# Window-attention maxima on one Trainium2 core: local and global scores in separate PSUM banks, the mask written by ScalarE

## The reference

```python
h = layernorm(x);  q, k, v = split(h @ w_qkv)
# local: a query in block n (64 tokens) sees the keys from 32 before it to 31 after it
logits = where(win & valid, q . k_neighbours * scale, -1e9)
out_local  = softmax(logits) @ v_neighbours
# global: every 64th token is a key for all queries of its sequence
out_global = softmax(q . k[::64] * scale) @ v[::64]
x = x + layernorm((out_local + out_global) @ w_out + b_out)
x = x + layernorm(real(ifft(fft(layernorm(x)) @ w)) + bias)
```

## Time and profile before

| | |
|---|---|
| median of 3 runs | 3774.73 us |
| the profiled execution, its own time | 3778.02 us |
| its span, first to last instruction | 3775.7 us |
| mean granted TensorE clock | 0.99 |
| busy: PE, PEld | 3697.7, 2682.5 us |
| busy: DVE, ACT, POOL | 2319.9, 1587.6, 1928.3 us |

### The profile page before, as it was taken

One profiled execution on the slowest core, in us unless ns is written; L12 is line 12 of the kernel. 1 busy time (PEld: TensorE's weight loads), 2 busy tenths in 40 slices (PEclk: granted clock), 3 DMA queues, 4 the chain that ended last, 5 costly groups with the idle time before them and its releaser, 6 DMA issues.

```text
span 3775.7 us, 77146 instructions
## 1 busy us (share of the span) xinstructions
PE 3697.7 (98%) x28480; PEld 2682.5 (71%) x28480; DVE 2319.9 (61%) x5331; ACT 1587.6 (42%) x3094; POOL 1928.3 (51%) x3087
## 2 busy tenths in 40 slices
PE   8999999999999899999999999999999999999997
PEld 6888888888874566666666666666666666666675
DVE  4333333333323567777777777777777777777774
ACT  3222222222220344555555555555555555555554
POOL 0000000000000367777777777777777777777777
PEclk9999999999999899999999999999999999999999
DMA  4554455445556456666666666666666666666651
GB/s 154 191 200 169 165 200 191 166 176 200 184 204 155 96 129 152 151 140 142 144 148 145 139 148 153 151 140 141 144 149 145 139 149 149 152 140 140 144 119 40
DMA packets 421938, 574.34 MB, mean 152 GB/s; under 512 B 41688, under 2 KB 186216, under 8 KB 421624
## 3 DMA queue, kind: packets, MB, share of 16 engines
q1 hardware_dynamic: 413080, 567.94, 57.1%
q10 hardware_dynamic: 8256, 2.16, 0.2%
q0 software_dynamic: 288, 0.08, 0.0%
HBM read 364.74 MB, written 203.23 MB: 150 GB/s over the span
## 4 chain that ended last, share of the span: by engine, by line
PE 62%; POOL 1%; ACTq 1%; ACT 0%; DVE 0%; issue 0%; POOLq 0%
PE ps_misc L995 19%; PE ps_max L915 10%; PE ps_sc L935 6%; PE ps_o L967 6%; PE ps_max L918 5%; PE ps_s L967 4%; PE ps_sc L949 4%; PE ps_o L979 3%; PE ps_s L973 3%; PE ps_sc L1004 1%; ACTq L782 1%; PE ps_sc L924 1%; PE ps_sc L943 1%; ACT qk L759 0%; POOL rsb L696 0%
## 5 line engine op out<-in xcount | busy, mean ns | idle before, releaser
L827 DVE TENSOR_REDUCE mx<-ps_max 128x2 f32<-128x256 f32 (+1 forms) x1365 | 485.0, 355 | 489.8 <-PE ps_max L918 466.7
L759 ACT ACTIVATE qk<-ps_sc 128x384 f32<-128x384 f32 (+1 forms) x1024 | 418.9, 461 | 666.0 <-PE ps_sc L935 663.3
L828 DVE TENSOR_REDUCE mx<-ps_max 128x2 f32<-128x384 f32 (+1 forms) x1365 | 612.6, 449 | 0.0
L915 PE MATMUL ps_max<-ks,qs 97*128 97x384 f32 x2048 | 569.1, 357 | 15.1 <-DVE mx L828 13.1
L915 PEld LDWEIGHTS ps_max<-ks,qs 97*128 97x128 f32 x2048 | 368.6, 192 | 180.9 <-DVE mx L828 127.1
L705 POOL TENSOR_SCALAR_AFFINE_SELECT qk<-qk 128x512 f32<-128x512 f32 (+1 forms) x512 | 298.5, 583 | 282.6 <-ACT qk L759 282.5
L371 PE MATMUL po<-ht_hi,w_hi 128*128 128x512 f32 x1024 | 405.6, 396 | 1.5 <-ACT ht_hi L248 1.5
L371 PE MATMUL po<-ht_hi,w_lo 128*128 128x512 f32 x1024 | 400.3, 391 | 0.0
L371 PE MATMUL po<-ht_lo,w_hi 128*128 128x512 f32 x1024 | 399.8, 390 | 0.0
L772 ACT ACTIVATE v<-ps_sc 128x512 f32<-128x512 f32 x512 | 298.2, 596 | 152.4 <-PE ps_sc L949 150.2
L918 PE MATMUL ps_max<-mask,ident_b 128*128 128x192 bf16 x2048 | 352.9, 254 | 0.0
(11 more groups left out here) (114 smaller groups left out, 7507.5 us busy)
## 6 DMA issues: line engine op xcount, KB each, us to landing
ks<-k_hi_d SPq DMA_DIRECT2D x256, 288.0 KB
qs<-q_hi_d SPq DMA_DIRECT2D x256, 256.0 KB
ks<-k_lo_d SPq DMA_DIRECT2D x128, 288.0 KB
xb<-in_L_attn_x SPq DMA_DIRECT2D x132, 256.0 KB, 3.5
q_lo_d<-o_lo SPq DMA_DIRECT2D x32, 1024.0 KB, 8.7
k_lo_d<-o_lo SPq DMA_DIRECT2D x32, 1024.0 KB, 10.1
qs<-q_lo_d SPq DMA_DIRECT2D x128, 256.0 KB
vw<-v_d SPq DMA_DIRECT2D x128, 256.0 KB, 2.9
```

The lines of the kernel that those rows point to most:

```text
L759: nc.scalar.activation(p_loc[:, i, 2 * hp:2 * hp + 2, lo:MW], ps_sc[n % 2][:, 0:2 * MW].rearrange("p (h n) -> p h n", h=2)[:, :, lo:MW], A ...
L827: nc.vector.tensor_reduce(mx[s % 2][:, 1, h:h + n, tile], ps_max[:, b:b + n, MW:MW + NGLOB], axis=AX.X, op=ALU.max)
L828: last = nc.vector.tensor_reduce(mx[s % 2][:, 0, h:h + n, tile], ps_max[:, b:b + n, 0:MW], axis=AX.X, op=ALU.max)
L915: nc.tensor.matmul(ps_max[:, b, 0:2 * MW], qs[g][0:ROWS_MAX, h, tile * P:(tile + 1) * P], both_keys(g, h, tile), start=True, stop=True)
```

## The change

The three-bank tile `ps_max` is replaced by two banks `ps_ml` for local scores (two heads of 192 columns in each, used in turn by even and odd units) and one bank `ps_mg` for global scores (two heads of 128 columns). A unit on PE becomes two local matmuls of 192 columns, which do not clear the bank but add to what is in it, and then two global matmuls of 128 columns; both pairs load the same two query tiles, so there are again four weight loads. The mask matmuls L918 are gone. In their place a new item `seed` on ACT copies the mask, for two heads at once (128 x 384 values), into the local bank as soon as DVE has reduced it; unit u+2 then adds its scores there. Two matmuls ahead of all units write the mask into the banks for units 0 and 1. DVE always takes both heads at once, first the local half, then the global half, and signals each by itself (`ml_taken`, `mg_taken`): PE's local matmuls of unit u wait for the seed that follows the local reduction of unit u-2, the global ones for the global reduction of unit u-1.

```diff
-        ps_max = pb("ps_max", [P, 3, 512])
+        ps_ml = [pb(f"ps_ml{b}", [P, 2, 256]) for b in range(2)]
+        ps_mg = pb("ps_mg", [P, 4, P])
...
-        MAXIMA = (-12.81, -11.26, -10.56, -9.74, -8.61, -7.49, -6.9, -6.1)
-        TAKEN = 0.12
-        SCORES = (("mt", 0, -4.23), ("loc", 0, -0.65), ("loc", 1, 0.87), ("loc", 2, 1.16), ("loc", 3, 5.18),
-                  ("last", 0, 5.77), ("glob", 0, 1.84), ("glob", 1, 2.44), ("glob", 2, 2.81), ("glob", 3, 5.4))
+        MAXIMA = (-12.98, -11.14, -10.52, -9.53, -8.35, -7.35, -7.13, -6.1)
+        TAKEN = 0.05
+        SEED = 0.55
+        SCORES = (("mt", 0, -3.77), ("loc", 0, -1.32), ("loc", 1, 0.5), ("loc", 2, 0.87), ("loc", 3, 5.22),
+                  ("last", 0, 5.74), ("glob", 0, 1.64), ("glob", 1, 2.01), ("glob", 2, 2.3), ("glob", 3, 5.48))
...
+                items += [(t + at + SEED, "seed", s, n) for n, at in enumerate(MAXIMA)]
...
@@ scalar
+                    u = 8 * s + i
+                    if name == "seed" and u + 2 < 8 * STEPS:
+                        act.wait_ge(ml_taken, u + 1)
+                        nc.scalar.activation(ps_ml[u % 2][:, :, 0:MW], mask[:].rearrange("p (o n) -> p o n", o=1).to_broadcast([P, 2, MW]),
+                                             ACT.Copy).then_inc(seeded, 1)
@@ vector
-                        dve.wait_ge(max_scored, u + 1)
-                        near = high - low == 1
-                        for b, h, n in ((low, 2 * pair, 2),) if near else ((low, 2 * pair, 1), (high, 2 * pair + 1, 1)):
-                            nc.vector.tensor_reduce(mx[s % 2][:, 1, h:h + n, tile], ps_max[:, b:b + n, MW:MW + NGLOB], axis=AX.X, op=ALU.max)
-                            last = nc.vector.tensor_reduce(mx[s % 2][:, 0, h:h + n, tile], ps_max[:, b:b + n, 0:MW], axis=AX.X, op=ALU.max)
-                        last.then_inc(max_taken, 1)
+                        dve.wait_ge(ml_scored, u + 1)
+                        nc.vector.tensor_reduce(mx[s % 2][:, 0, heads, tile], ps_ml[u % 2][:, :, 0:MW], axis=AX.X,
+                                                op=ALU.max).then_inc(ml_taken, 1)
+                        dve.wait_ge(mg_scored, u + 1)
+                        nc.vector.tensor_reduce(mx[s % 2][:, 1, heads, tile], ps_mg[:, 0:2, :], axis=AX.X,
+                                                op=ALU.max).then_inc(mg_taken, 1)
@@ tensor
+                for b in range(2):
+                    nc.tensor.matmul(ps_ml[b][:, :, 0:MW], ident_b[:],
+                                     mask[:].rearrange("p (o n) -> p o n", o=1).to_broadcast([P, 2, MW]), start=True, stop=True)
...
-                        for n, b in enumerate((first, second)):
-                            h = 2 * pair + (b == high)
-                            at_least(pe, max_taken, u - 1 + n)
-                            nc.tensor.matmul(ps_max[:, b, 0:2 * MW], qs[g][0:ROWS_MAX, h, tile * P:(tile + 1) * P],
-                                             both_keys(g, h, tile), start=True, stop=True)
-                        for b in (first, second):
-                            last = nc.tensor.matmul(ps_max[:, b, 0:MW], ident_b[:], mask[:], start=False, stop=True, skip_group_check=True)
-                        last.then_inc(max_scored, 1)
+                        queries = [qs[g][0:ROWS_MAX, 2 * pair + n, tile * P:(tile + 1) * P] for n in range(2)]
+                        keys = [ks[g][0:ROWS_MAX, 2 * pair + n, :] for n in range(2)]
+                        at_least(pe, seeded, u - 1)
+                        for n in range(2):
+                            last = nc.tensor.matmul(ps_ml[u % 2][:, n, 0:MW], queries[n], keys[n][:, tile * P:tile * P + MW],
+                                                    start=False, stop=True, skip_group_check=True)
+                        last.then_inc(ml_scored, 1)
+                        at_least(pe, mg_taken, u)
+                        for n in range(2):
+                            last = nc.tensor.matmul(ps_mg[:, n, :], queries[n], keys[n][:, SPAN:KROW], start=True, stop=True)
+                        last.then_inc(mg_scored, 1)
```

More of the change, by code:

```diff
@@ L580, in attention_phase @@
         y_stored = [sem(f"y_stored{i}") for i in range(TILES)]
-        max_scored, max_taken = sem("max_scored"), sem("max_taken")
+        seeded, ml_scored, ml_taken = sem("seeded"), sem("ml_scored"), sem("ml_taken")
+        mg_scored, mg_taken = sem("mg_scored"), sem("mg_taken")
         sc_scored, sc_exped = sem("sc_scored"), sem("sc_exped")
@@ new lines, in attention_phase @@
+        TAKEN = 0.05
+        SEED = 0.55
+        SCORES = (("mt", 0, -3.77), ("loc", 0, -1.32), ("loc", 1, 0.5), ("loc", 2, 0.87), ("loc", 3, 5.22),
+                  ("last", 0, 5.74), ("glob", 0, 1.64), ("glob", 1, 2.01), ("glob", 2, 2.3), ("glob", 3, 5.48))
+        VALUES = (("pvl", 0, 3.43), ("pvl", 1, 4.14), ("pvl", 2, 7.23), ("pvl", 3, 7.49), ("pvl", 4, 7.98),
+                  ("pvgs", 0, 8.07), ("oc", 0, 8.66), ("sums", 0, 8.91), ("pvgo", 0, 9.2), ("rglob", 0, 9.06),
+                  ("og", 0, 9.62), ("rloc", 0, 13.95), ("ol", 0, 14.07), ("osum", 0, 14.1))
@@ new lines, in attention_phase @@
+        LATE = (("ot", (24.09, 20.31, 19.06, 15.22)), ("otl", (22.15, 22.4, 20.11, 15.25)))
+        OUT_AT = ((8.8, 9.72, 10.39, 10.6), (8.36, 8.94, 9.48, 10.1))
+        FFN_AT = ((24.77, 25.8, 25.91, 26.74), (25.01, 25.41, 25.93, 26.12))
+        TAIL = (("outa", (10.14, 10.48)), ("outs", (10.97, 10.7)), ("rs0", (12.14, 12.25)), ("y", (12.45, 14.89)),
+                ("ya", (13.22, 16.29)), ("x1", (16.27, 17.22)), ("rs1", (16.46, 17.65)), ("x1n", (17.85, 18.74)),
+                ("tr", (19.38, 19.68)), ("trl", (20.87, 20.26)), ("ffna", (26.47, 26.35)), ("ffns", (27.13, 28.5)),
+                ("rs2", (29.09, 29.52)), ("z", (33.77, 35.43)), ("za", (34.1, 35.47)))
@@ L644, in attention_phase @@
         MISC_BEFORE = dict(zip(MISC[1:], MISC[:-1]))
-        def max_banks(u):
-            first, second = 2 * u % 3, (2 * u + 1) % 3
-            return first, second, min(first, second), max(first, second)
         with nc.Block() as block:
@@ L819, in item @@
                         u = 8 * s + i
-                        tile, pair = i // 2, i % 2
-                        low, high = max_banks(u)[2:]
+                        tile, heads = i // 2, slice(2 * (i % 2), 2 * (i % 2) + 2)
                         if i == 0 and s > 1:
                             dve.wait_ge(sc_scored, unit(s - 2, "mt", 0) + 1)
-                        dve.wait_ge(max_scored, u + 1)
-                        near = high - low == 1
-                        for b, h, n in ((low, 2 * pair, 2),) if near else ((low, 2 * pair, 1), (high, 2 * pair + 1, 1)):
-                            nc.vector.tensor_reduce(mx[s % 2][:, 1, h:h + n, tile], ps_max[:, b:b + n, MW:MW + NGLOB], axis=AX.X, op=ALU.max)
-                            last = nc.vector.tensor_reduce(mx[s % 2][:, 0, h:h + n, tile], ps_max[:, b:b + n, 0:MW], axis=AX.X, op=ALU.max)
-                        last.then_inc(max_taken, 1)
+                        dve.wait_ge(ml_scored, u + 1)
[4 more added lines that the diff above has]
+                                                op=ALU.max).then_inc(mg_taken, 1)
                     if name == "sums":
@@ L908, in item @@
                         tile, pair = i // 2, i % 2
-                        first, second, low, high = max_banks(u)
                         if i == 0:
                             pe.wait_ge(st_loaded[g], 160 * (s // GROUPS + 1))
-                        for n, b in enumerate((first, second)):
-                            h = 2 * pair + (b == high)
-                            at_least(pe, max_taken, u - 1 + n)
-                            nc.tensor.matmul(ps_max[:, b, 0:2 * MW], qs[g][0:ROWS_MAX, h, tile * P:(tile + 1) * P],
-                                             both_keys(g, h, tile), start=True, stop=True)
-                        for b in (first, second):
-                            last = nc.tensor.matmul(ps_max[:, b, 0:MW], ident_b[:], mask[:], start=False, stop=True, skip_group_check=True)
-                        last.then_inc(max_scored, 1)
+                        queries = [qs[g][0:ROWS_MAX, 2 * pair + n, tile * P:(tile + 1) * P] for n in range(2)]
[9 more added lines that the diff above has]
+                        last.then_inc(mg_scored, 1)
                     if name == "mt":
@@ L922, in item @@
                         bank_free(n)
-                        pe.wait_ge(max_taken, 8 * s + 8)
+                        pe.wait_ge(mg_taken, 8 * s + 8)
                         nc.tensor.transpose(ps_sc[n % 2][0:8 * TILES, 0:P], mx[s % 2][:].rearrange("p a h t -> p (a h t)"),
```

3 lines of the change are left out of this document (removed).

## The result

The changed kernel takes 3760.34 us, median of 6 runs (3749.61 to 3763.78), beside 3777.36 us for the kernel before (3774.47 to 3780.58, 6 runs). The ratio is 0.9949, 95% interval 0.9933 to 0.9964. It is faster by 17 us where 102 were forecast, and lies outside the range. The profiled execution took 3760.2 us, its span is 3758.4 us.

A forecast was written before the change was run, and what follows sets the result against it. PE's own instructions were taken to bound the steady step. Units -102 us, first units -10 and late moments +10 sum to -102 us, from a profiled span of 3775.7 to 3674; median forecast 3673 us, range 3640 to 3730.

The forecast's parts named there:

- PE's unit: On PE: four matmuls at 0.109, 0.436 us a unit instead of 0.54, over 1024 units -102 us.
- The rival in which the stream sets the turn: On PE: weight loads hidden, 640 columns take 0.30 us a unit; 246 us less, 3529 us, chance 0.04.
- exposed loads: On PE: each pair of matmuls exposes its first load, 0.59 us a unit; 3826 us, chance 0.02.
- What bounds the kernel: Steady step: nothing but PE's own instructions sets the pace; PE busy 998 of 1000 us.
- The start of the phase: First 12 units, PE and DVE taking turns: 1.1 us apart instead of 1.9, -10 us.
- DVE and the price of a seed: DVE: 100 us less busy time from two-head instructions, no gain by itself; ACT: 0.49 us a seed.
- ACT is hidden: ACT: seeds add 3.9 us a step, 15.0 of 18.4 us with DMA issues (82%), hidden on its own.
- the whole sum: Whole kernel: -102 - 10 + 10 = -102 us, median 3673 us, chance 0.71.
- the other moves in the table cost nothing: Due times, with the two mask matmuls at the start: same instructions, same tile-width switches, so no cost.
- 10 us for rare late moments: ACT late or a DMA issue of up to 1.92 us not hidden: +10 us, bounds 0 and +63.
- The walk: One step followed through ACT, DVE and PE: seeds ready 1 us or more ahead, tightest spare 0.3 us.
- half given back: One 0.49 us seed a step delays an exponential PE needs: +63 instead of +10, 3726 us, chance 0.14.

The follow-up runs named there:

- the old table: Changed kernel with all due times of the kernel before, plus seeds 0.55 after their maxima: 3662.55 us (0.9696).

## Why the prediction was wrong

**PE's unit: right in kind, too dear.** Local (192 columns) and global (128) take the same 0.20 us a pair, so the columns do not set the turn of these small float32 matmuls. That the weight load sets it fits, but no run changes the load alone. I took 0.109 from the score pass; it is 0.10. By the shares of the chain with the old table, (10.1% + 8.3%) of 500 us for 500 / 18.43 x 8 = 217 units, a unit with its switches costs 0.424 us, 0.560 before. That is 0.136 less a unit, 1.1 us a step, where the step itself fell by 0.86: the rest went to other blocks. The rival in which the stream sets the turn (0.30) fell, and so did exposed loads (0.59). The Trainium skill's 81 ns for a load and matmul at 128 columns (TensorE: Matmul & The Clock Gate, section Back-to-back issue gap) is below the 100 ns seen here.

**What bounds the kernel: nearly right.** I read that nothing but PE sets the pace of a steady step. Without the DMA issues on ACT's queue the kernel before was 21 us faster, so PE had small waits already.

**The start of the phase: right for the first units.** 1.21 us a unit for 1.1. What follows them had no term: from 1230 to 1300 us the granted clock is 0.60 in the changed kernel, 0.75 before, some 10 us at full clock.

**DVE and the price of a seed: right.** 494 ns for 490, and 111 us less in DVE's reductions (1098 to 986) for 100.

**ACT is hidden: right for the seeds, in the old order.** With that the whole sum can be tested: it gives 3673 us for the change without its new due times, and the run of that kernel took 3663. The sum holds to 10 us because two errors met: the units brought more than their term, and other blocks took some of it (L951, by its share, 1.27 us a step for 1.17).

**The failed step is the table.** The prediction put it as "the other moves in the table cost nothing: same instructions, same switches between tile widths", and gave back 10 us for rare late moments. The new due times cost 98 us in this kernel and 53 in the kernel before, the larger part of it as PE's wait for the exponentials of `loc3` before `glob3`. The walk that should have found it went through one step, the one with `ffn`; the loss lies in the others, where `y`, `outs`, `ot` and one `out` had changed sides with `loc3` or `maxr0`. I had written that ACT is fuller in steps with `tr`, `y` and `x1n`, and did not walk through them.

**The rival that came true in part** is half given back: 3726 us from one late exponential a step, chance 0.14. Its place was right (a `ps_sc` bank that waits for ACT) and its cause was not: I priced one seed of 0.49 us; it was a chain of a reduction, a seed, a copy, two issues and a norm. The condition was there to be read: 1.1 us of DMA issues between `mt` and `loc3` is in the earlier trace rows, and I used it for the landing of the data and for ACT's load, never for what stands behind it.

## What to carry to other kernels

Where each engine follows a written order, the order is part of the change: sort the old and the new table for every kind of step, and list which items have changed sides with one that PE waits for, before pricing anything. Total load does not show it: ACT had 500 us more to do and hid them all in one order, and lost 43 us by them in the other. And count a DMA issue as an instruction on the engine that issues it: here each of the two took some 0.55 us of ACT's queue, and what stood behind them waited. Put it on a queue on which nothing urgent stands behind.

## What the runs showed of the hardware

**A short wait and the clock.** In the changed kernel PE's clock fell at times in the steady part, which it did not do in the kernel before: mean 0.981 against 0.990. One place (columns as in the earlier trace rows, granted clock third from the end):

```profile
2720.00:2730.00 10.00, 10.00 (x92) 7.82 (x88) 7.48 (x18) 6.62 (x15) 7.61 (x13) 1.00 0.93 227
2730.00:2740.00 10.00, 8.63 (x65) 6.41 (x63) 4.61 (x10) 5.11 (x12) 6.84 (x10) 0.73 0.48 104
2740.00:2750.00 10.00, 10.00 (x57) 6.16 (x55) 5.05 (x11) 3.61 (x8) 5.63 (x11) 0.50 0.64 142
2750.00:2760.00 10.00, 9.24 (x76) 7.39 (x73) 6.30 (x13) 6.28 (x13) 2.30 (x4) 0.91 0.13 39
```

```profile
2732.66 0.50 PE L951 MATMUL ps_sc<-qs,ks 99*128 99x512 f32 x1 [1.37 <-ACT qk L758]
```

PE stood still for 1.37 us before `glob3`, after 30 us without a gap; then the clock goes to the lower of its two levels (0.50, 1.2 GHz) for some 17 us, in which each turn nearly doubles. The fall begins at about 2734.6 and the three windows hold 5.4 + 10 + 1.8 us of it. The length of the wait does not decide it. From 1450 to 3660 us PE waits 29 times for 1.18 us or more before `glob3`, and three of these waits were followed by a fall: the longest (1.66 us, at 1965.60), this one, and one of 1.19 us, after which the clock was low for some 7 us. A longer one, 1.31 us, was not followed by any; the clock there stays at 1.00:

```profile
2043.32 0.50 PE L951 MATMUL ps_sc<-qs,ks 99*128 99x512 f32 x1 [1.19 <-ACT qk L758]
...
2351.22 0.50 PE L951 MATMUL ps_sc<-qs,ks 99*128 99x512 f32 x1 [1.31 <-ACT qk L758]
```

```profile
2045.00:2050.00 5.00, 5.00 (x42) 3.85 (x44) 2.84 (x6) 2.62 (x6) 4.79 (x7) 0.52 0.79 177
...
2350.00:2500.00 150.00, 145.39 (x1435) 109.66 (x1436) 111.08 (x237) 103.77 (x222) 115.73 (x182) 1.00 0.65 148
```

What these runs don't show is what decides. But a stall can cost more than its length. The means differ by 0.009 of 3758 us, 34 us of full clock; some 18 of them lie between 1230 and 1450 us, at the start of the phase (0.60 for 0.75 over 70 us, 0.92 for 0.97 over 150). Most of the rest lies in two windows, 1900 to 2050 us (0.97) and 2650 to 2800 (0.94), where the kernel before has 1.00. The six runs of the changed kernel go with it: the two at 3750 and 3752 us have a mean clock of 0.987 and 0.986, the four at 3760 to 3764 us 0.981 to 0.983. No run holds the clock fixed; the steps at a clock of 1.00, above, give the waits alone.

**ACT writing to PSUM.** A copy of 128x384 from SBUF to PSUM took 494 ns, an exponential of the same size from PSUM to SBUF 488. The Trainium skill (ScalarE: Activation LUTs, section Step-by-step: what each stage is for) holds that writing PSUM is faster than writing SBUF. It does not show here, though the two differ in source and function as well.

**DMA issues on an engine's queue** took 0.51 to 1.92 us for the same small transfer. On SyncE they were as long (0.50 to 1.91 us), but no exponential stands behind them.
